# Latent attention's queries and outputs as three 16-bit products, outputs in the queries' banks, and the tail of each pair in another order

## The reference

```python
x = x + experts(layernorm(x))                     # step 3
h = layernorm(x)                                  # step 4, for each of 8 sequences of 128 rows
q = ((h @ Wqa) @ Wqb)                             # 256 -> 192 latents -> 16 heads of 64 + 64 (rotary)
c_kv, k_pe = split(h @ Wkva)                      # 64 latents, 64 rotary
k, v = split(c_kv @ Wkvb)                         # 16 heads: keys of 64, values of 128
p = softmax(causal((q_nope @ k + rope(q_pe) @ rope(k_pe)) * 128 ** -0.5))
x = x + concat(p @ v) @ Wo
```

## Time and profile before

| | |
|---|---|
| times of 3 runs | 722.07, 720.9, 721.73 us; median 721.73 |
| the profiled execution | 726.51 us, span 724.7 us |
| busy share of the span | PE 77%, weight loads 54%, DVE 60%, ACT 41%, POOL 35% |
| mean granted TensorE clock | 0.888 of full speed |
| chain that ended last | PE 51%, DVE 17%, POOL 14%, ACT 10%, issue 4%, DMA 3% |
| step 3 (experts) | about 200 to 344 us of the span |
| step 4 (latent attention) | about 344 to 563 us; one pair every 47 us |

### The profile page before, as it was taken

One profiled execution on the slowest core, in us unless ns is written; L12 is line 12 of the kernel. 1 busy time (PEld: TensorE's weight loads), 2 busy tenths in 40 slices (PEclk: granted clock), 3 DMA queues, 4 the chain that ended last, 5 costly groups with the idle time before them and its releaser, 6 DMA issues.

```text
span 724.7 us, 12063 instructions
## 1 busy us (share of the span) xinstructions
PE 557.3 (77%) x4143; PEld 393.3 (54%) x4143; DVE 431.7 (60%) x994; ACT 299.9 (41%) x742; POOL 254.1 (35%) x297
## 2 busy tenths in 40 slices
PE   3948799157279999999869989899888367763665
PEld 2537444155158888887525656576576246543243
DVE  3586899955635555554672534535455646767773
ACT  1512200242634444443423735627364355645553
POOL 3950488855600000000676935909512200010000
PEclk9979899755679999999978999999999799985886
DMA  8592310545651111110320000000000500000000
GB/s 292 176 374 91 137 59 0 165 150 200 202 176 45 46 46 45 46 45 24 94 73 1 1 0 1 1 1 0 1 1 1 174 2 2 2 2 0 7 23 30
DMA packets 32248, 49.62 MB, mean 68 GB/s; under 512 B 3096, under 2 KB 22368, under 8 KB 31808
## 3 DMA queue, kind: packets, MB, share of 16 engines
q1 hardware_dynamic: 29888, 41.65, 17.3%
q0 software_dynamic: 2304, 7.21, 2.8%
HBM read 39.68 MB, written 9.18 MB: 67 GB/s over the span
## 4 chain that ended last, share of the span: by engine, by line
PE 51%; DVE 17%; POOL 14%; ACT 10%; issue 4%; DMA 3%; SPq 0%; ACTq 0%; DVEq 0%; POOLq 0%
PE bank L1560 14%; PE bank L1723 4%; PE bank L1575 4%; POOL sm L524 3%; POOL rq L517 3%; POOL sorted_rows L499 3%; POOL qs L519 2%; POOL rq L515 2%; PE bank L1438 2%; ACT pT L819 2%; PE bank L1467 2%; PE bank L1469 2%; PE bank L1468 2%; PE bank L1867 2%; PE bank L1968 1%
## 5 line engine op out<-in xcount | busy, mean ns | idle before, releaser
L667 ACT ACTIVATE hf<-bank,be 128x256 f32<-128x256 f32 (+1 forms) x120 | 44.3, 420 | 69.0 <-PE bank L1560 53.6
L505 POOL DMA_INDIRECT yg<-expert_rows,pos x16 | 15.8, 989 | 156.0 <-DMA expert_rows<-yb 151.5
L1560 PE MATMUL bank<-h,wsp 128*128 128x256 f16 (+1 forms) x720 | 67.3, 249 | 1.7 <-DVE h L1118 1.6
L1560 PEld LDWEIGHTS bank<-h,wsp 128*128 x720 | 57.2, 97 | 10.9 <-issue 4.5
L1116 DVE CAST h<-hf 128x512 f16<-128x512 f32 (+1 forms) x60 | 21.8, 364 | 56.6 <-ACT hf L667 55.3
L487 POOL TENSOR_TENSOR kvp<-xnT,cxT 128x512 f32<-128x512 f32 x32 | 35.6, 1135 | 43.0 <-issue 33.1
L722 ACT ACTIVATE sm<-sm,nm 128x128 f32<-128x128 f32 x128 | 49.7, 393 | 1.0 <-DVE nm L1231 1.0
L577 ACT CAST wsp<-wraw 128x2048 f16<-128x2048 f32 x12 | 22.6, 1900 | 65.7 <-DMA wraw<-in_L_ffn_W 65.7
L465 POOL TENSOR_TENSOR wsp<-wraw,wsp 128x512 f16<-128x512 f32 x40 | 45.6, 1176 | 9.0 <-ACT wsp L577 8.7
L1228 DVE SCALAR_TENSOR_TENSOR sm<-bank,const 128x512 f32<-128x512 f32 x32 | 22.1, 692 | 38.9 <-PE bank L1690 38.9
L524 POOL TENSOR_TENSOR sm<-sm,rinv 128x512 f32<-128x512 f32 x32 | 33.1, 1040 | 26.0 <-DVE rinv L1222 26.0
(11 more groups left out here) (299 smaller groups left out, 1327.6 us busy)
## 6 DMA issues: line engine op xcount, KB each, us to landing
wraw<-in_L_ffn_W SPq DMA_DIRECT2D x16, 512.0 KB, 5.2
wraw<-in_L_ffn_W SPq DMA_DIRECT2D x8, 1024.0 KB, 6.1
cxT<-in_ctxT SPq DMA_DIRECT2D x2, 1024.0 KB, 7.5
tap<-in_taps SPq DMA_DIRECT2D x1, 2048.0 KB, 14.1
xg<-sorted_rows SPq DMA_DIRECT2D x8, 256.0 KB, 2.9
expert_rows<-yb SPq DMA_DIRECT2D x8, 256.0 KB, 2.2
sorted_rows<-early POOLq DMA_DIRECT2D x1, 1536.0 KB, 12.0
sorted_rows<-early POOLq DMA_DIRECT2D x1, 1408.0 KB, 14.9
```

Of the source, the lines that this page charges most:

```text
L667: last = nc.scalar.activation(hf[:, p, n * k:n * k + n], bank[2 * (layer - 1) + p][:, n * k:n * k + n], ACT.Gelu, bias=be[:, layer - 1, u, ...
L1560: last = nc.tensor.matmul(b[:, n * (f % 2):n * (f % 2) + n], w[a_][:, c, P * f:P * f + P], inp[:, b_, c, :], start=(c == 0 and a_ + b_ == ...
```

## The change

The queries' weights `wqb`, the query latents `ql`, the outputs' operands `oT` and the folded output weights `wvo` become 16-bit pairs (hi and lo), and both products three 16-bit products. The lo parts are made by DVE (`latents_low`, `heads_low`, and four subtractions for `wvo`), those of `wqb` by POOL. The rotary weights, until now loaded to where they are used, are loaded over `wab` and split from there. `output` writes banks 1 and 2 (the queries') and not bank 7. In the tail the first tile's output stands ahead of two transposes on PE, ACT copies the first tile's heads ahead of its last exponentials, and DVE splits heads between its copies. Semaphores that step 3 used (`h1_lo`, `h2_lo`) go on counting in step 4 from `TILE_LOWS`. Most of the lines around the edits are left out. The hunks stand in the order of the file: places in memory, SP, POOL (418 and 498), ACT (677 to 756), DVE (1092 to 1281), PE (from 1517):

```diff
@@ -113,13 +113,16 @@
...
-        wo4a = sb("wo4a", [P, H4 // 2, D])
-        wvo = wo4a
+        s4o = ExitStack()
+        wo4a = sb("wo4a", [P, H4 // 2, D], F32, s4o)
+        s4o.close()
+        wvo = sb("wvo", [P, H4 // 2, 2, D], F16)
...
+        rope_wab = wab
@@ -241,7 +244,7 @@
...
-        wqb = sb("wqb", [P, 3, 2, 8, 64], F32, sq4)
+        wqb = sb("wqb", [P, 2, 3, 2, 8, 64], F16, sq4)
@@ -256,8 +259,7 @@
...
-        ql0 = sb("ql0", [P, 2, P], F32, s4)
-        ql1 = sb("ql1", [P, 2, P], F32, s4)
+        ql = sb("ql", [P, 2, 2, 2, P], F16, s4)
@@ -273,7 +275,7 @@
...
-        oT = sb("oT", [P, 2, H4 // 2, P], F32, s4)
+        oT = sb("oT", [P, 2, 2, H4 // 2, P], F16, s4)
@@ -311,6 +313,7 @@
...
+        TILE_LOWS = 2 * ET
@@ -339,7 +342,7 @@
...
             for k, b in enumerate((6, 7, 5, 6)):
-                yield wvo[:, 2 * k:2 * k + 2, :].rearrange("p j n -> p (j n)"), bank[b][:]
+                yield wvo[:, 2 * k:2 * k + 2, 0, :], bank[b][:].rearrange("p (j n) -> p j n", j=2)
@@ -418,12 +421,13 @@
...
             sp.wait_ge(sem("w_split_dve"), 6)
-            sp.dma_start(wqb[:, :, 1].rearrange("p c h n -> p c (h n)"), a["wqb_rope"].rearrange("p (c n) -> p c n", c=3)).then_inc(sem("w4_loaded"), 16)
             sp.dma_start(wkvT[:], a["wkvT"].rearrange("(c p) n -> p c n", p=P)).then_inc(sem("context5_loaded"), 16)
...
             sp.wait_ge(sem("wab_moved"), 1)
+            sp.dma_start(wab[:].rearrange("p c h n -> p c (h n)"), a["wqb_rope"].rearrange("p (c n) -> p c n", c=3)).then_inc(sem("w4_loaded"), 16)
+            sp.wait_ge(sem("wab_moved"), 3)
             sp.dma_start(cxT[:].rearrange("p c t s -> p (c t s)"), a["ctxT"]).then_inc(sem("cxT_loaded"), 16)
             for j in range(ET):
@@ -498,6 +502,14 @@
...
+            fold, turn = (wqb[:, :, :, half].rearrange("p a c h n -> p a c (h n)") for half in range(2))
+            staged = wab[:].rearrange("p c h n -> p c (h n)")
+            pool.wait_ge(sem("w_hi"), 13)
+            nc.gpsimd.tensor_tensor(fold[:, 1], staged, fold[:, 0], ALU.subtract).then_inc(sem("wab_moved"), 1)
+            pool.wait_ge(sem("w4_loaded"), 48)
+            nc.gpsimd.tensor_copy(turn[:, 0], staged).then_inc(sem("wab_moved"), 1)
+            pool.wait_ge(sem("wab_moved"), 2)
+            nc.gpsimd.tensor_tensor(turn[:, 1], staged, turn[:, 0], ALU.subtract).then_inc(sem("wab_moved"), 1)
             pool.wait_ge(sem("y0_stored"), 16 * (ET // 2 + 2))
@@ -677,7 +689,7 @@
...
-            nc.scalar.copy(wqb[:, :, 0].rearrange("p c h n -> p c (h n)"), wab[:].rearrange("p c h n -> p c (h n)")).then_inc(sem("wab_moved"), 1)
+            nc.scalar.copy(wqb[:, 0, :, 0].rearrange("p c h n -> p c (h n)"), wab[:].rearrange("p c h n -> p c (h n)")).then_inc(sem("w_hi"), 1)
             for j in range(ET):
@@ -709,8 +721,7 @@
...
-                nc.scalar.copy(ql0[:].rearrange("p u s -> p (u s)"), bank[0][:, 0:2 * P])
-                nc.scalar.copy(ql1[:].rearrange("p u s -> p (u s)"), bank[0][:, 2 * P:4 * P]).then_inc(sem("lat_copied"), 1)
+                nc.scalar.copy(ql[:, 0].rearrange("p w u s -> p (w u s)"), bank[0][:]).then_inc(sem("lat_copied"), 1)
             def key_latents(i, u):
@@ -745,14 +756,19 @@
...
-                exps(i, 1, 2)
-                exps(i, 1, 3)
-                for u in range(2):
+                def heads_out(u):
...
-                        nc.scalar.copy(oT[:, u, 4 * k:4 * k + 4, :].rearrange("p h n -> p (h n)"), bank[7 if k == 0 else 0][:]).then_inc(sem("oT_ready"), 1)
-                    if after is not None:
-                        key_latents(after, u)
+                        nc.scalar.copy(oT[:, u, 0, 4 * k:4 * k + 4, :].rearrange("p h n -> p (h n)"), bank[7 if k == 0 else 0][:]).then_inc(sem("oT_ready"), 1)
+
+                exps(i, 1, 2)
+                heads_out(0)
+                exps(i, 1, 3)
+                if after is not None:
+                    key_latents(after, 0)
+                heads_out(1)
+                if after is not None:
+                    key_latents(after, 1)
@@ -1092,9 +1108,12 @@
...
+            for k, (hi, b) in enumerate(list(prep4_moves())[4:]):
+                dve.wait_ge(sem("prep4_act"), k + 5)
+                nc.vector.tensor_tensor(wvo[:, 2 * k:2 * k + 2, 1, :], b, hi, ALU.subtract).then_inc(sem("b3_added"), 1)
             split_low(14)
...
-            dve.wait_ge(sem("b3_added"), 4)
+            dve.wait_ge(sem("b3_added"), 8)
@@ -1151,7 +1170,7 @@
             def add_tile(i, u):
...
-                nc.vector.tensor_tensor(xt, xt, bank[7][:, 0:D], ALU.add).then_inc(sem("x4_added"), 1)
+                nc.vector.tensor_tensor(xt, xt, bank[1 + u][:, 0:D], ALU.add).then_inc(sem("x4_added"), 1)
@@ -1169,6 +1188,16 @@
...
+
+            def latents_low(i):
+                dve.wait_ge(sem("lat_copied"), i + 1)
+                nc.vector.tensor_tensor(ql[:, 1].rearrange("p w u s -> p (w u s)"), bank[0][:], ql[:, 0].rearrange("p w u s -> p (w u s)"),
+                                        ALU.subtract).then_inc(sem("h1_lo"), 1)
+
+            def heads_low(i, u, k):
+                dve.wait_ge(sem("oT_ready"), i * 4 + (2 * u + k + 1))
+                hi, lo = (oT[:, u, part, 4 * k:4 * k + 4, :].rearrange("p h n -> p (h n)") for part in range(2))
+                nc.vector.tensor_tensor(lo, bank[7 if k == 0 else 0][:], hi, ALU.subtract).then_inc(sem("h2_lo"), 1)
@@ -1190,6 +1219,8 @@
...
                 normalise(4, 4 + i, 2 * i, 2 * i + 2)
+                if i == 1:
+                    latents_low(0)
@@ -1229,14 +1260,19 @@
...
                     nc.vector.tensor_reduce(nm[:, u, hs], sm[:, u, hs, :], AX.X, ALU.max, negate=True).then_inc(sem("nm_ready"), 1)
+                    if j == 0 and after is not None:
+                        latents_low(after)
...
                         copy_pT(i, j - 3)
...
                 invert(i, 7)
-                for j in range(5, 8):
-                    copy_pT(i, j)
+                copy_pT(i, 5)
+                for half in range(2):
+                    heads_low(i, 0, half)
+                copy_pT(i, 6)
+                copy_pT(i, 7)
@@ -1245,6 +1281,9 @@
...
                         rope_k(after, u)
                     add_tile(i, u)
+                    if u == 0:
+                        for half in range(2):
+                            heads_low(i, 1, half)
@@ -1517,13 +1556,15 @@
...
             for k, b in enumerate((6, 7, 5, 6)):
...
+                if k == 3:
+                    pe.wait_ge(sem("b3_added"), 5)
...
-            pe.wait_ge(sem("b3_added"), 4)
+            pe.wait_ge(sem("b3_added"), 8)
@@ -1615,7 +1656,7 @@
...
-            pe.wait_ge(sem("wab_moved"), 1)
+            pe.wait_ge(sem("wab_moved"), 3)
@@ -1656,17 +1697,23 @@
             def queries_low(i, j):
...
+                if j == 0 and i >= 2:
+                    pe.wait_ge(sem("x4_added"), 2 * i - 1)
...
-                    pe.wait_ge(sem("lat_copied"), i + 1)
+                    pe.wait_ge(sem("h1_lo"), TILE_LOWS + i + 1)
...
-                for k in range(2):
-                    a_, rows = 4 * (j % 4 // 2), slice(64 * k, 64 * k + 64)
-                    nc.tensor.matmul(four_heads(bank[1 + k][:]), ql1[rows, u, :], wqb[rows, 2, :, a_:a_ + 4, :].rearrange("p w h n -> p h w n"), start=True, stop=False)
+                for a, w in passes:
+                    for k in range(2):
+                        a_, rows = 4 * (j % 4 // 2), slice(64 * k, 64 * k + 64)
+                        nc.tensor.matmul(four_heads(bank[1 + k][:]), ql[rows, a, 1, u, :], wqb[rows, w, 2, :, a_:a_ + 4, :].rearrange("p w h n -> p h w n"),
+                                         start=(a + w == 0), stop=False)
             def queries_high(i, j):
...
-                nc.tensor.matmul(four_heads(bank[1 + k][:]), ql0[:, u, :], wqb[:, k, :, a_:a_ + 4, :].rearrange("p w h n -> p h w n"),
-                                 start=False, stop=True).then_inc(sem("q4_psum"), 1)
+                for a, w in passes:
+                    last = nc.tensor.matmul(four_heads(bank[1 + k][:]), ql[:, a, 0, u, :], wqb[:, w, k, :, a_:a_ + 4, :].rearrange("p w h n -> p h w n"),
+                                            start=False, stop=(a == 1))
+                last.then_inc(sem("q4_psum"), 1)
@@ -1702,11 +1749,12 @@
...
             def values(i, u, after):
-                pe.wait_ge(sem("x4_added"), i * 2 + (u + 1))
+                if i + u:
+                    pe.wait_ge(sem("h2_lo"), TILE_LOWS + CREDIT + i * 4 + 2 * u)
...
-                    pe.wait_ge(sem("oT_ready" if u else "kT_ready"), i * 4 + 2 if u else i + 1)
+                    pe.wait_ge(sem("h2_lo" if u else "kT_ready"), TILE_LOWS + CREDIT + i * 4 + 2 if u else i + 1)
...
-                    pe.wait_ge(sem("lat_copied"), after + 1)
+                    pe.wait_ge(sem("h1_lo"), TILE_LOWS + after + 1)
@@ -1718,9 +1766,14 @@
             def output(i, u, lo, hi):
```

(17 more changed lines are left out.)

## The result

The changed kernel takes 746.04 us (median of 4 runs, 742.54 to 749.62), 1.031 of the kernel before with an interval of 1.026 to 1.036. The forecast was 737 with a range of 728 to 743: slower, as said, but by 24 us and not by 15. The profiled execution took 748.73 us (span 746.9), 22.2 more than the profiled one of before. A second profile of each kernel was taken later (spans 749.7 and 721.5), to see which parts repeat.

A forecast was written before the change was run, and what follows sets the result against it. In step 4 POOL's stretch, then mostly PE, bounds each pair; in step 3 PE does. 12.0 - 2.3 + 4.8 - 1.8 + 2.8 = +15.5 on the median 721.73 gave 737 us, range 728 to 743.

The forecast's parts named there:

- Step 3: Start of step 3: SP's row loads queue behind POOL's staging of split weights and PE waits; +12.0 us (10.3 to 14).
- `wvo`'s subtractions: Ahead of step 3: four DVE subtractions and PE's wait on one are covered; zero, 1.7 us without that cover.
- Queries in 16 bit: Step 4: low rows' passes take 0.80 us for 1.06; all but each pair's first group lie hidden under POOL's step.
- The prologue: Prologue, where queries are on the chain: quicker 16-bit products save time; -2.3 us (-3.1 to 0).
- The first queries: Each next pair's first queries wait for `latents_low` and reach POOL 1.6 us later; +4.8 us (3.8 to 6.3) over three pairs.
- The tails: Tails of pairs 0 to 2: output 0 moved earlier mostly misses PE's hole, waiting on DVE; -1.8 us (-8 to +3).
- The last pair: Last pair: ACT's last exponentials come later, PE stands for `heads_low`, output 1 ends later; +2.8 us (1.8 to 3.7).
- The first rival: Step 3: staging is over in time, tile 2's rows land before 219.56, the 12.0 falls away; 725.2 us, chance 0.06.
- the third rival: Queries and outputs: three 16-bit products are no quicker than one f32 product; +25.6, 747 us, chance 0.06.
- The second rival: Tails and last pair: output 0 runs in PE's hole, saving 4.9 us each, 19.6 in all; 716.6 us, chance 0.05.

The follow-up runs named there:

- the first experiment: Changed kernel with SP issuing the next tiles' row loads ahead of its two waits for POOL's staging; 740.52 us, 1.018 of the kernel before.
- the experiment: Changed kernel with DVE's subtraction for the latents' lo parts ahead of the first scores' mask of each pair; 743.52 us, 1.025 of the kernel before.
- heads first, weights late and the rest: Changed kernel with row loads early, POOL's staging in pieces, latents' and heads' lo parts earlier, step 5's weights later on DVE; 709.57 us, 0.976 of the kernel before.

## Why the prediction was right or wrong

**Step 3: right, +12.0 of 12.0**, by the mechanism named. The exact figure is luck in part, as the single prices were off and cancelled: POOL's 1536-wide instructions took 3.10, 1.46 and 3.14, not 3.5, 1.9 and 3.5, the staging began 1.2 later, and PE stood 9.63 where 10.5 was reckoned. What the prediction did not see is the second cost beneath. It weighed the Trainium skill's page "SBUF — State Buffer", section "Who interferes with whom", and then took a quarter of an instruction from the earlier trace rows as the price, on POOL's side. The rows of the first experiment show the price on DVE's side, and the whole of POOL's instruction: 0.43 became 3.27. In that section the Trainium skill calls the shared port an exclusive lock, held for a whole instruction, and the rows agree. The earlier trace rows showed a price of 0.18; taking the queueing away alone would have brought 7.2 and not 12.

**`wvo`'s subtractions: zero, not contradicted.** Step 3's first transposes start at 200.28 and 197.41, at 199.85 and 201.02 before.

**Queries in 16 bit: right in size.** Six passes of the low rows take 0.82 at full clock (0.80 taken), where the f32 pair took 1.06. They are hidden as said: POOL's stretch of pair 1 is 27.49 before and 27.53 after, in the first profiles.

**The prologue: not settled.** -2.3 was taken out of a quarter of seven rows, 3.1; but four records like those of the first row (2.01) take 1.06 in the earlier trace rows, and the granted clock was 0.50 behind that row and 1.00 at the last. So a part of the saving read from them holds only while the clock is low. The second profile of before has this stage 3.2 us shorter without any change. The difference of the means, with the 1.6 of the first queries in it, is +0.6, in a scatter of that size.

**The first queries: right, +1.6 a pair.** The stop of 2.15 less what PE saves; the experiment took 1.6 of it away in each of three pairs. What the prediction gave no price is the low clock behind this stop. In pair 0 both profiles show it (six passes of low rows in 1.44 and 1.39, for 0.82 at full clock); in pairs 1 and 2 it is the 0.99 and 1.15 us of the second profile.

**The tails: wrong, and the main miss.** The step that failed is "the last `copy_pT` at 475.9, where tile 1's values start". `values` waits for `kvr_ready` as well, and DVE makes that by the rotation, behind step 5's weights. The prediction had both numbers (2.2 and 0.85) in its next sentence, but let them hold only the heads of tile 1. By its own rows the values start at 475.9 + 2.2 + 0.85 = 479.0, three later; the measured stops are 2.97, 3.50 and 1.90. In pair 1 of the changed kernel these values start 8.9 us behind the end of the last division but one, where the forecast had 6.2. (469.72, which the prediction takes for the end of the last division, is that of the last but one: POOL's row of the last two goes from 468.67 to 470.71.)

The first queries' 3.2 taken off, the three pauses grew by 3.5 on the mean, where -1.8 was forecast. Part of the new stops would not have shown, since output 1 waits for DVE anyway: without the clock, the pauses grew by 2.4 to 4.3, of which 3.2 are the first queries and -1.8 was to be the tails. The clock is the other part. The forecast counted one fall a tail, as in the earlier trace rows, and 1.5 us for it; with stops ahead of output 0 and of the values the clock took 6.4 and 10.0 us of three pauses, where it took 5.0 and 4.7 (1.2 of the 10.0 stand behind the third stop). So of the 5.3 us above the forecast the clock has some 3.4 on the mean and the waits 1.9; in the first profile alone the waits have the larger part, 2.8 of 4.4.

**The last pair: right in kind, 1.1 short.** The forecast lay between 2.1 at full clock and 3.8 with a fall; it was the fall in both profiles (output 0 took 4.42 and 4.18, not 2.78), and 41.5 less 37.4 is 4.1, 41.2 less 37.4 is 3.8. POOL's stretch itself became 2.1 longer (16.88 against 14.77), as ACT's last exponentials stand behind the heads and the last division behind them.

**The rivals.** The first rival, a staging that is over in time, fell with the 9.63 us that PE stood for tile 2's rows. Three 16-bit products are quicker than one f32 product here (0.82 to 1.06 for the low rows; at full clock 24 products of an output in 2.78, where the 16 f32 records of the last pair took 3.62), so the third rival gave the nearest time by another road. The second rival, output 0 off the path, was a real possibility that the change's order of DVE prevents: with heads first, weights late and the rest it came true, 709.6, with 4.2 to 4.5 us off each of the three pauses and 2.8 off the last, where that rival reckoned 4.9 for each.

**What the range missed.** It stopped at 743, with the tails' upper end at +3 for three pairs. Their pauses gave 5.3 more than forecast, most of it on the mean a price (the clock) of which the earlier trace rows had one sample. With them alone the forecast would have become 742, still inside. The last pair's 1.1 and the 1.2 of the clock in POOL's stretches bring it to some 745; what is left, -1.6, +1.3 and +2.4 in the first, third and last row of the table, is not told from scatter.

## What to carry to other kernels

When an instruction is moved earlier, list what it was covering: every engine's work that ran beside it, and who waits for that; here output 0 had covered the weights and the keys on DVE. Price a stop of PE as two terms, the wait and the slow products behind it, and do not take one profile's clock for either kernel's. Do not let a queue that feeds the critical engine wait for a chain on a slow one, and when that wait is taken away, look for a collision that the wait had hidden.

## What the runs showed of the hardware

A POOL instruction held a DVE instruction off for its whole length: 0.43 became 3.27 beside one of 3.09, and in the other order a POOL copy of 0.61 took 1.16 beside a DVE subtraction. It touched a DVE cast with one input as well (0.29 to 1.55). The Trainium skill's page "SBUF — State Buffer", section "Who interferes with whom", counts casts among the instructions that can take the shared port, when in a fast mode; this row agrees that a cast can be held off, though no row names its mode.

The same stops of PE did not have the same effect on the clock from one execution to the next. With 2.13 and 1.90 us of standing in pair 2, the granted clock stayed at 1.00 in one profile of the changed kernel and cost 1.4 us in the other; with 2.15 and 2.97 in pair 0 of the one, 2.14 and 2.96 of the other, it cost 4.7 and 1.7 up to the next pair's first queries. In the one kernel whose tails had no stop above 1.42 us, it did not fall in any of the three, in its one profile.
